# A post-norm decoder layer on one core: the first item's convolution, the bias pieces, the centroids and the loads of up_w at new places in the start-up

## The reference

```python
# 1. a complex decay c per channel; the sequence axis is the ITEM axis (32 steps)
gamma = exp(-exp(lmlg)); c = gamma * exp(1j * theta)
conv[n] = sum_{m<=n} c**(n-m) * x[m]  +  last_conv * c**(n+1)
x = layernorm(x + conv.real * x)
# 2. cross attention, 16 heads of 16 channels, relu on the projections
Q = relu(x @ Wq + bq); K = relu(ctx @ Wk + bk); V = relu(ctx @ Wv + bv)
out = softmax(Q K^T / 4) V + Q
x = layernorm(x + (ln_g * norm(out) + ln_b))
# 3. each token goes to the nearest of 8 centroids' expert
xn = rms_norm(x) * scale
ids = argmin_e(|xn|^2 + |centroid_e|^2 - 2 xn . centroid_e)
a, g = split(xn @ up_w[ids]); y = (a * silu(g)) @ down_w[ids]
x = layernorm(x + y + x)
```

## Time and profile before

| | |
|---|---|
| Median of 3 runs | 1278.97 us (1272.46 to 1282.16) |
| The profiled execution | 1285.39 us, its span 1283.3 us |
| Busy share of the span | PE 87%, DVE 74%, POOL 62%, ACT 52% |
| Granted TensorE clock, mean | 0.935 of full speed |
| First scores matmul (start of step 0) | 56.31 us |
| Phase 1, then phase 2 | to about 866 us, then to the end |

### The profile page before, as it was taken

How to read it: one execution, slowest core, us unless ns; L and a number is a source line. 1 busy time by engine, 2 the same in 40 slices (tenths; PEclk the granted TensorE clock), 3 DMA queues, 4 the chain that set the end, 5 groups by cost and what they waited for, 6 DMA issues and landing times. The chain is left out here.

```text
span 1283.3 us, 27523 instructions
## 1 busy us (share of the span) xinstructions
PE 1114.9 (87%) x8060; PEld 817.8 (64%) x8061; DVE 953.8 (74%) x2411; ACT 664.2 (52%) x1413; POOL 792.0 (62%) x943
## 2 busy tenths in 40 slices
PE   0599999999999998999999999830999999999996
PEld 0465666666666666666666666520788888888885
DVE  6357799899899899899899898639455555555553
ACT  1247577676677677776776677514322222222221
POOL 6545778888788888888887865344133333333333
PEclk9859899999899999999999999755999999999998
DMA  5556755655556646656556555206011111111110
GB/s 143 131 158 173 189 144 143 154 138 150 141 142 149 160 130 153 151 146 155 142 146 152 141 134 128 76 25 180 25 53 49 44 52 49 52 46 47 53 49 22
DMA packets 90827, 144.92 MB, mean 113 GB/s; under 512 B 12663, under 2 KB 78336, under 8 KB 84513
## 3 DMA queue, kind: packets, MB, share of 16 engines
q1 hardware_dynamic: 84192, 126.61, 38.3%
q0 software_dynamic: 6528, 16.99, 4.5%
HBM read 91.44 MB, written 53.03 MB: 113 GB/s over the span
## 5 line engine op out<-in xcount | busy, mean ns | idle before, releaser
L888 DVE TENSOR_REDUCE neg_max_sb<-S 128x2 f32<-128x512 f32 x512 | 327.9, 682 | 78.6 <-PE S L693 77.6
L559 ACT ACTIVATE probs<-T 128x512 f32<-128x512 f32 x512 | 278.5, 595 | 152.4 <-PE T L706 140.5
L693 PE MATMUL S<-k_st,q_st 48*128 48x256 f32 x1024 | 215.4, 320 | 51.5 <-DMA k_st<-k_pieces 26.0
L693 PEld LDWEIGHTS S<-k_st,q_st 48*128 48x128 f32 x1024 | 146.7, 193 | 131.1 <-issue 56.3
L706 PE MATMUL T<-q_st,k_st 49*128 49x256 f32 x1024 | 210.5, 318 | 3.7 <-ACT probs L559 2.1
L706 PEld LDWEIGHTS T<-q_st,k_st 49*128 49x128 f32 x1024 | 145.6, 192 | 21.0 <-ACT probs L559 16.2
L1201 ACT ACTIVATE gT<-GT 128x512 f32<-128x512 f32 x71 | 42.6, 600 | 207.5 <-PE GT L1236 207.5
L669 PE MATMUL O<-probs,v_aug 128*32 128x256 f32 x2048 | 147.1, 408 | 0.7 <-ACT probs L559 0.7
L1177 POOL DMA_INDIRECT out<-res,token x71 | 76.4, 1076 | 101.5 <-DVE res L1309 101.5
L1258 PE MATMUL Y<-dn_sb,gT 128*128 x568 | 134.2, 379 | 0.8 <-ACT gT L1201 0.8
L513 POOL DMA_INDIRECT buckets<-row,slot x64 | 66.2, 1034 | 90.4 <-DVE slot L1052 80.2
(11 more groups left out here) (177 smaller groups left out, 2551.6 us busy)
## 6 DMA issues: line engine op xcount, KB each, us to landing
q_st<-q_pieces SPq DMA_DIRECT2D x64, 256.0 KB, 4.7
k_st<-k_pieces SPq DMA_DIRECT2D x64, 256.0 KB, 5.9
xr<-buckets SPq DMA_DIRECT2D x71, 129.0 KB, 2.1
xt<-in_x SPq DMA_DIRECT2D x32, 256.0 KB, 6.4
ct<-in_ctx SPq DMA_DIRECT2D x32, 256.0 KB, 6.8
up_sb<-in_L_ffn_up_w SPq DMA_DIRECT2D x8, 1024.0 KB, 8.6
q_pieces<-q_hi SPq DMA_DIRECT2D x32, 256.0 KB, 2.1
q_pieces<-q_lo SPq DMA_DIRECT2D x32, 256.0 KB, 2.1
```

Of the source, the lines that this page charges most:

```text
L559: a_.activation(probs[:, h % 8].rearrange("p k t -> p (k t)"), T_ps[h % 2][:, :], ACT.Exp, scale=DH ** -0.5).then_inc(s["exp_ok"], 1)
L693: last = t_.matmul(S_ps[h % 2][:, c * TOK:(c + 1) * TOK], q_st[base:base + STACK, h, c * P:(c + 1) * P], k_st[base:base + STACK, h, :], st ...
L888: v.tensor_reduce(neg_max[:, cur.mod(2), :, h], S_ps[h % 2][:, :].rearrange("p (c t) -> p c t", c=NTC), AX.X, ALU.max, negate=True).then_i ...
```

## The change

The diff, cut to its core:

```diff
-PARAMS = 13
-UP_STEPS = (-2, -1, 0, 1, 2, 3, SEQ - 1, SEQ)
+PARAMS = 11
+BIAS = 18
+UP_STEPS = (0, 1, 2, 3, 4, 5, SEQ - 1, SEQ)
...
# SyncE
                 def read_k(item, half):
+                    if item.k == 0:
+                        sp.wait_ge(s["fill"], 2)
...
-                    sp.dma_start(state[:, 0, c, :], bcast(last_conv)).then_inc(s["params"], 16)
+                    sp.dma_start(state[:, 0, c, :], bcast(last_conv)).then_inc(s["past_in"], 16)
...
# GpSimd
+                g.memset(ones_bf[:, :], 1.0).then_inc(s["setup_pool"], 1)
...
-                g.memset(k_st[:, :, :].bitcast(F32), 1.0).then_inc(s["setup_pool"], 1)
-                g.memset(v_aug[:, :, :, :], 1.0).then_inc(s["setup_pool"], 1)
...
                 def conv_products(item):
...
                     wait(pool, "conv", item - 1, 5)
+                    if item.k == 1:
+                        wait(pool, "x1_ok", item - 1, 2)
...
-                    cut(n, q32[:, :, :], q_hi, q_lo, "q_ok", "q_cut", q_out)
+                    if n.k > 0:
+                        cut(n, q32[:, :, :], q_hi, q_lo, "q_ok", "q_cut", q_out)
... (the same for k)
-                conv_products(Item(0, 0))
-                conv_real(Item(0, 0))
-                conv_imag(Item(0, 0), 0)
-                conv_imag(Item(0, 0), 1)
-                conv_input(Item(0, 0))
                 steps(pool, step)
...
# ScalarE
+                act.wait_ge(s["setup_pool"], 1)
+                a_.activation(v_aug[:, :, :, :].rearrange("p r k w -> p (r k w)"),
+                              ones_bf[:, 0:1].to_broadcast([P, 4 * NTC * (H * VW + 32 - VW)]), ACT.Copy).then_inc(s["fill"], 1)
... (behind the two sines)
+                a_.activation(k_st[:, :, :].rearrange("p h t -> p (h t)"),
+                              ones_bf[:, 0:1].to_broadcast([P, H * TOK]), ACT.Copy).then_inc(s["fill"], 1)
...
# TensorE
-                pe.wait_ge(s["params"], PARAMS * 16)
-                pe.wait_ge(s["setup_pool"], 14)
-                ... (centroids: transposes, wait, sums)
-                pe.wait_ge(s["setup_dve"], SETUP_DVE)
+                def centroid_flip():
+                    wait(pe, "qn_ok", Item(0, 0))
+                    ... (the transposes, into M_ps[2])
+                def centroid_norms():
+                    pe.wait_ge(s["setup_dve"], CENT_SQ)
+                    ... (the sums, into M_ps[2])
...
+                        if h == 2 and n.k == 0:
+                            pe.wait_ge(s["params"], PARAMS * 16)
+                            pe.wait_ge(s["setup_pool"], 12)
+                        if h == 3 and cur.k == 0:
+                            centroid_flip()
+                        if h == 9 and cur.k == 0:
+                            centroid_norms()
... (V's first row, h == 11)
+                                if n.k == 0:
+                                    pe.wait_ge(s["setup_dve"], BIAS)
... (h == 14)
+                            if n.k == 1:
+                                pe.wait_ge(s["setup_dve"], SETUP_DVE)
...
# VectorE: the bias and the centroids leave the set-up and become functions
+                def first_state():
+                    both = [P, 2, NTC, C]
+                    re_b = decay_re.unsqueeze(1).to_broadcast([P, NTC, C])
+                    pair_b = decay[:, :, :].unsqueeze(2).to_broadcast(both)
+                    dve.wait_ge(s["past_in"], 2 * 16)
+                    dve.wait_ge(s["setup_pool"], 12)
+                    v.tensor_tensor(by_re[:, :, :, :], state[:, 0].unsqueeze(1).to_broadcast(both), pair_b, ALU.mult).then_inc(s["conv"], 1)
+                    dve.wait_ge(s["conv"], 1)
+                    v.tensor_tensor(state[:, 0], by_re[:, 1], state[:, 1], ALU.subtract).then_inc(s["conv"], 1)
+                    ... (times re_b, plus by_re[:, 0])
+                    dve.wait_ge(x_in[0], 16)
+                    dve.wait_ge(s["conv"], 4)
+                    v.tensor_tensor(state[:, 0], state[:, 0], xt[:, 0], ALU.add).then_inc(s["conv"], 1)
+                def bias_pieces():
+                    dve.wait_ge(s["params"], PARAMS * 16)
+                    ... (the seven operations of before)
+                def centroids_scaled():
+                    dve.wait_ge(s["setup_pe"], 1)
+                    ... (four operations)
+                def centroids_squared():
+                    dve.wait_ge(s["setup_pe"], 2)
+                    ... (cent_norm)
+                def first_cuts():
+                    wait(dve, "q_ok", Item(0, 0), 4)
+                    v.tensor_tensor(q_lo[:, :, :], q32[:, :, :], q_hi[:, :, :].bitcast(F32), ALU.subtract).then_inc(s["q_cut"], 1)
+                    wait(dve, "k_ok", Item(0, 0), 4)
+                    v.tensor_tensor(k_lo[:, :, :], k32[:, :, :], k_hi[:, :, :].bitcast(F32), ALU.subtract).then_inc(s["k_cut"], 1)
...
+                    if t.k == -2:
+                        first_state()
...
+                        if h == 14 and t.k == -2:
+                            bias_pieces()
+                        if h == 1 and t.k == -1:
+                            first_cuts()
+                        if h == 5 and t.k == 0:
+                            centroids_scaled()
+                        if h == 11 and t.k == 0:
+                            centroids_squared()
```

More of the change, by code:

```diff
@@ new lines, in bias_pieces @@
+                def bias_pieces():
+                    dve.wait_ge(s["params"], PARAMS * 16)
+                    for k in range(3):
+                        at = slice(32 * k, 32 * k + 1)
+                        setup(v.tensor_copy(bv_cut[at, :].rearrange("p (c d) -> p c d", c=NTC), bv_bc[at, :].unsqueeze(1).to_broadcast([1, NTC, C])))
+                        if k < 2:
+                            setup(v.tensor_copy(bv_bf, bv_bc))
+                            setup(v.tensor_tensor(bv_bc, bv_bc, bv_bf, ALU.subtract))
+                    assert done[0] == BIAS
@@ new lines, in centroids_scaled @@
+                def centroids_scaled():
+                    dve.wait_ge(s["setup_pe"], 1)
+                    ctv = centT[:, :, :].rearrange("p o e -> p (o e)")
+                    setup(v.tensor_scalar(ctv, M_ps[2][:, 0:NCH * E], -2.0, None, ALU.mult))
+                    setup(v.scalar_tensor_tensor(cent_sq[:, :, :].rearrange("p o e -> p (o e)"), ctv, 0.25, ctv, ALU.mult, ALU.mult))
+                    assert done[0] == CENT_SQ
+                    for o_ in range(NCH):
+                        setup(v.tensor_scalar(centT[:, o_], centT[:, o_], scale_col[:, o_:o_ + 1], None, ALU.mult))
```

49 lines of the change are left out of this document (18 added, 31 removed).

## The result

After the change the kernel takes 1275.65 us (median of 20 runs, 1264.97 to 1282.01); the kernel before took 1283.09 (median of 20 runs beside them, 1272.46 to 1296.7). The ratio is 0.9936, with a 95% interval of 0.9912 to 0.996: 7.4 us less, where 15.2 were forecast, and 1275.65 lies above the range that ended at 1274. Two exact copies of the changed kernel, compared again later, gave 0.9885 [0.9844, 0.9927] and 0.9905 [0.9862, 0.9949]. Taken together, 80 executions of the kernel before and 35 of the changed one have means of 1284.67 and 1272.85: 11.8 us less, with a standard error of 1.1.

What follows compares the result with a forecast made beforehand. TensorE bounds step 0, so the start of the first scores decides: 17.4 us sooner, less 1.4 for the centroids and 0.8 for the moved loads, gives 15.2 off 1278.97, so 1263.8 us; range 1253 to 1274.

Steps and rivals of the forecast that it cites:

- a lead won at 56.31 should arrive whole at the end: After step 0: any time by which the first scores start sooner, forecast 17.4 us, reaches the end undiminished.
- the centroids in step 0: Centroid matmuls moved from set-up into TensorE's step 0 at half clock: cost 1.4 us, bounds 0.9 to 2.2.
- against the median of the runs, 1278.97: Base of the sum: 15.2 us taken from the runs' median 1278.97, giving 1263.8, not from the profiled 1285.39.
- The angle chain and the convolution on VectorE: Set-up: L836 takes 0.35 us instead of 3.94; first convolution 4.2 us against 8.16 on GpSimd; u starts at 14.0.
- they land by 16.66 at the latest: Set-up: the parameters GpSimd's rstd waits for land by 16.66, so x1 starts between 17.05 and 17.75, taken 17.3.
- x1 without item 1's products: Set-up: with by_re held, x1's two halves take 0.8 us instead of 3.77; x1 ends at 18.1 against 34.19.
- Bias, cuts and the way to DRAM: Before step 0: bias ends at 27.1, k's lower piece written at 31.3, then 7.63 us to first scores at 38.9.
- The moved loads: Two megabytes of up_w moved from set-up to steps 4 and 5: cost 0.8 us for both, bounds 0 and 8.
- The rival of late waits: Steps 4 and 5 both meet the K stack reads badly, with clock falls: 8.0 us gained, 1271; chance 0.2.
- early clock: Rival: the clock rises within step 0's first third, worth 8 us, giving 1256; chance 0.15.
- late landing: Rival: x or past state delays VectorE's convolution to 14 or later, costing 4 us, giving 1268; chance 0.08.
- slower: Rival: half clock through steps 1 and 2 makes the kernel slower than before, 1294 at 60 us more; chance 0.03.

Runs made afterwards that it cites:

- GpSimd's convolution: Changed kernel with item 0's convolution back on GpSimd, ahead of the wait for the parameters: 1276.66 us, ratio 0.9916 to the kernel before.
- products not held: Changed kernel without the wait that holds GpSimd's products of item 1 until item 0's x1 is written: 1276.65 us, ratio 0.993 to the kernel before.
- wait moved: Changed kernel with GpSimd's wait for the parameters put behind item 0's rstd, at the start of step 0: 1269.94 us, ratio 0.9888.
- In the gap instead: Changed kernel with the centroid pieces moved from step 0 to the end of step -1: 1274.73 us, ratio 0.9897 to the kernel before.
- filled gap: 38 constant matmuls added on TensorE before step 0: in the changed kernel 1265.61 us, ratio 0.9841; in the kernel before 1283.45 us, ratio 0.998.
- fills alone: Kernel before with only k_st and v_aug filled by ScalarE: 1287.64 us against 1287.66, ratio 1.0.

## Why the prediction was wrong

The start-up went as forecast: the first scores came 16.1 to 16.8 us sooner. Two steps of the sum failed. One is its base, 1278.97, where 80 executions have a median of 1284.2. The other is "a lead won at 56.31 should arrive whole at the end": of the 16.1 to 16.8 us the executions together show 11.8, with an error of 1.1, and the centroids in step 0, for which the sum had 1.4, account for 0.6 of what is missing. For the rest, some 4 us, step 8 has a likely part (2.2, the clock), and its cause stays open. Of the 11.9 us between 1263.8 and 1275.65, 5.2 are the base, 3.4 are the gain (15.2 against 11.8), and the last 3.3 are the luck of the first comparison: its 20 executions of the changed kernel lie that far above the median of all 35, 1272.3, which is inside the range. Taken by the first comparison alone, the base accounts for 4.1 and the gain for 7.8. The steps in order:

1. **"against the median of the runs, 1278.97"** is, over all executions, where the forecast lost most. I took the median of three runs, 1278.97, and kept the profiled execution's 6.4 us above it as its own. The 80 runs have a median of 1284.2: the profiled execution (1285.39) was the typical one and the three runs were the lucky ones. This alone puts the forecast 5 us too low (4 by the first comparison's own 20). With a standard deviation of 5 us a mean of three is good to 3; I had named the spread of 9.7 us and used it for the border of 1% and for "some luck" in the range, not for the choice of the base. By the profiled execution the same sum gave 1270.2.
2. **The angle chain and the convolution on VectorE**: forecast 0.35 and 4.2, measured 0.29 and 4.2; u forecast at 14.0, measured 13.86. Right.
3. **"they land by 16.66 at the latest"** is the first step in order of time that failed. The start of L407 is one landing out of a scatter: the kernel before and its edits have 15.7 to 17.0, and in the changed kernel, which issues item 2's x and context at 14.57, beside the parameters, they landed at 17.10, 16.47 and 16.29. x1 started at 18.18, 17.56 and 17.37, against 17.3. That is up to 0.9 us.
4. **x1 without item 1's products**: the duration was right (0.74 for both, where 0.8 was forecast), the worth was not told apart from the rest. Taking the hold out gives it 1.4 us.
5. **Bias, cuts and the way to DRAM**: bias forecast to end at 27.1 from 18.15, measured 18.83 to 27.76, so the 8.9 us under contention held. The write of k's lower piece came at 31.94 against 31.3. The last leg, 7.63 us by the old trace, took 8.30, and 8.1 to 8.6 in every trace of the changed kernel and its edits. Most of that is the event from which the leg was measured: before, k's lower piece was written 0.87 behind its upper one, now 0.46, and from the upper one's write to the first scores are 8.76 us against 8.50. With the 0.6 by which the write came late this is the whole difference between 38.9 and 40.24. (A slip of reading without effect: ahead of u at 27.38 TensorE had done the sums of the earlier trace rows too, not only the two transposes.)
6. **The centroids in step 0**, 1.4 us: in the changed kernel's trace their two pieces on TensorE took

```profile
45.59 0.38 PE L643 MATMUL M<-ident,probs 8*128 8x8 f32 x2
...
55.48 0.61 PE L650 MATMUL M<-cent_sq,ones_r 128*128 128x8 f32 x4
```

so 1.0 (1.4 in the copies, whose sums took 1.02). What they cost is read where the clock hardly differs: in three edited kernels with 36.3 to 36.5 us at 1.2 GHz in this part (GpSimd's convolution, products not held, wait moved) the way from the first scores to the end of step 1 took 50.54, 50.64 and 50.56, against 49.98 and 36.0 us before. That is 0.6, of which the clock may have up to 0.3. In the gap instead they brought nothing that could be measured.
7. **The moved loads**, 0.8 us: nothing, and perhaps 1 us gained at the start, which was inside the lead. The rival of late waits (1271) is nearer the measured time than the forecast and is refuted in its mechanism: the kernel before with the loads moved runs at 1.0002, and the changed one with the loads back at 0.9903 against 0.9885.
8. **What no step had**: the lead was to arrive whole, with the clock as it was. The mean half-clock time rose from 161.6 to 169.4 us, and at 0.28 us each this takes 2.2 us. That the change causes the rise isn't shown: it rests mostly on the first 20 executions, and in the two groups where both kernels have a clock the difference is -2 and +9 us. The traces don't place it either. In the rest, behind step 29, the changed kernel and its copies have 99 to 112 us against 92 before and are 1.3, 7.3 and 1.1 us longer; but the kernel before with the filled gap has 99 there too, and the changed one with the old loads 96. The long stretch at 1.2 GHz near the end of phase 1 has 27.3 us in the changed kernel and its copies (from 792 in the first) and 23.9 before (from 815); why is open.

At an equal half-clock time of 160 us the fit puts the three sets of the kernel before at 1283.6, 1283.9 and 1286.1 and those of the changed one at 1271.2, 1269.0 and 1268.9: means weighted by runs 1284.7 and 1270.2, a gain of 14.5. So lead 16.1 to 16.8, less 0.6 for the centroids, gives 15.5 to 16.2; less 2.2 for the clock 13.3 to 14.0; the runs say 11.8 with an error of 1.1. What is left, 1.5 to 2.2 us, lies within twice that error, and no experiment here can tell it from chance. The first comparison (7.4 by medians, 8.6 by means) is the low end of a scatter that the later ones (means 15.3 and 12.5 less, each with an error of 2 to 2.4) show.

Of the rivals, the **early clock** was the one that mattered. The clock came back 15 us behind the first scores in this trace, 8 us behind them in the copies (where it fell again from 50 to 68), and 33 us behind them with the wait moved. The copies thus met this rival's condition, a rise within the first third of step 0; what that is worth is at most 2.7 us up to the end of step 1 (50.56 against 47.89) and not 8, since the clock fell again. With the gap before step 0 filled it is 3.0 to 4.5 us. The Trainium skill, page "TensorE: Matmul & The Clock Gate", section "What's actually happening", says that activity releases the throttle; the windows with 13.40 of 14.00 us busy at 0.50 do not agree, and the filled gap agrees in the changed kernel's trace and not in that of the kernel before. The **late landing** of x or the past state did not occur: the convolution started at 9.62. The **slower** rival, half clock through steps 1 and 2, did not either: no trace has it longer than some 33 us behind the first scores, where the kernel before has 32.5.

## What to carry to other kernels

Before a gain is summed, take the base from as many executions as its scatter wants, and ask of the profiled one where in that scatter it lies; its mean granted clock is a first hint. A landing time read from one trace is one draw (15.9 to 17.0 here with the same loads in the queue), and a change that lets other loads start sooner may move it as well. A leg of the path that begins with two writes is longer from the second one when the two come closer together (0.4 of the 0.7 us here). A chain that is shortened in front of a wait for DMA is worth nothing until its consumer moves ahead of that wait (fills alone, ratio 1.0), and a contention that is taken from one operation often meets the next one on the same engine (the hold, 1.4 of 3.0).

## What was unexpected on the hardware

- The granted clock sits at 1.2 GHz for 8 to 33 us behind the first scores, with TensorE busy nearly all the time (13.40 of 14.00 us in the changed kernel, 18.64 of 19.00 in the filled kernel before), and how long differs between executions of the same instructions (15 us in the changed kernel's first trace, 8 in its copies, with a second fall from 50 to 68). In mean it moves the whole time by 0.28 us per microsecond, in steps bound by TensorE by 0.54.
- Filling the gap kept the clock up in one kernel's trace (3.4 us of half-clock time in the 19 us of step 0) and not in the other's (down for 31 us), where 1.48 us of idling were left before the first scores. Whether that rest is the cause was not tried, and the mean half-clock times (19 and 13 us less than beside them) say that a single trace overstates the contrast.
- Small operations on VectorE can be longer beside GpSimd as large ones are: the two scalings of 128x8 took 1.57 us together beside its convolution, 0.50 in the changed kernel's step 0. The seven operations on V's bias (three of 1x512, four of 128x256), which I had estimated at 3.0 us without company, took 8.9 beside it; with the products not held its convolution ended at 25.3, and the three operations behind that took 0.29, 0.42 and 0.42.
